# Decay exponents of the state-space pairs from stored running sums, inner products on row halves, and a new order inside a pair

## The reference

```
proj = u @ W_in.T                       # x|B|C (a causal convolution of 4 taps), z, A_log
a = -softplus(A_log).transpose(0, 2, 1) # one value per head and token
Lm = exp(segsum(a))                     # exp of the sum of a over (s, l], 0 for s > l
M = einsum('bhln,bhsn,bhls->bhls', Cm, Bm, Lm)   # C_l . B_s times the decay
y = einsum('bhls,bshp->blhp', M, x) + D * x
out = (y * silu(z + z_bias)) @ W_out.T
```

## Time and profile before

| | |
|---|---|
| median of 3 runs | 3554.8 us (3554.54 to 3561.59) |
| span of the profiled execution | 3547.7 us |
| PE busy | 3232.7 us, 91% |
| DVE busy | 2239.9 us, 63% |
| ACT busy | 1250.3 us, 35% |
| POOL busy | 1253.6 us, 35% |
| mean granted TensorE clock | 0.948 |

### The profile page before, as it was taken

How to read it: one execution, slowest core, us unless ns; L and a number is a source line. 1 busy time by engine, 2 the same in 40 slices (tenths; PEclk the granted TensorE clock), 3 DMA queues, 4 the chain that set the end, 5 groups by cost and what they waited for, 6 DMA issues and landing times.

```text
span 3547.7 us, 59609 instructions
## 1 busy us (share of the span) xinstructions
PE 3232.7 (91%) x20900; PEld 2219.6 (63%) x20900; DVE 2239.9 (63%) x2937; ACT 1250.3 (35%) x1904; POOL 1253.6 (35%) x1629
## 2 busy tenths in 40 slices
PE   3699989999789999999978999999997999899998
PEld 3445467777565447777655445777775454677775
DVE  1456676666646668666664766766665566776666
ACT  1133334444213323444412332444421333244442
POOL 1211114666221101666611111266642011146662
PEclk7789999999879999999987999999998899999999
DMA  7322101001212200011122320101112211011111
GB/s 244 104 66 54 36 12 34 30 30 36 75 48 54 65 13 24 29 30 30 31 78 54 71 49 1 30 30 32 35 35 78 65 43 48 10 30 36 30 36 45
DMA packets 121655, 166.69 MB, mean 47 GB/s; under 512 B 32224, under 2 KB 66656, under 8 KB 120864
## 3 DMA queue, kind: packets, MB, share of 16 engines
q1 hardware_dynamic: 117632, 151.11, 15.5%
q0 software_dynamic: 2720, 10.49, 0.7%
q10 hardware_dynamic: 1152, 3.15, 0.4%
HBM read 85.76 MB, written 19.92 MB: 30 GB/s over the span
## 4 chain that ended last, share of the span: by engine, by line
PE 79%; DVE 7%; issue 3%; DMA 3%; ACT 3%; SPq 2%; POOL 1%; ACTq 0%; DVEq 0%; POOLq 0%
PE ps L619 13%; PE ps L621 12%; PE ps L620 12%; PE ps L763 7%; PE ps L903 7%; PE ps L728 6%; PE ps L746 5%; PE ps L805 3%; PE ps L890 3%; PE ps L664 2%; PE ps L957 2%; DVE LM L1448 1%; PE ps L912 1%; DVE mneg L1374 1%; PE ps L629 1%
## 5 line engine op out<-in xcount | busy, mean ns | idle before, releaser
L619 PE MATMUL ps<-uh,win 128*128 128x512 f32 x1536 | 634.0, 413 | 0.0
L621 PE MATMUL ps<-uh,win 128*128 128x512 f32 x1536 | 604.1, 393 | 0.0
L620 PE MATMUL ps<-ul,win 128*128 128x512 f32 x1536 | 600.8, 391 | 0.0
L1374 DVE TENSOR_REDUCE mneg<-ps 128x1 f32<-128x128 f32 (+7 forms) x512 | 363.3, 752 | 174.9 <-PE ps L731 169.2
L1084 ACT ACTIVATE PR<-ps 128x1024 f32<-128x1024 f32 (+3 forms) x384 | 310.6, 810 | 405.8 <-PE ps L749 268.8
L1435 DVE SCALAR_TENSOR_TENSOR Bt<-ps,cpt,Bt 128x1023 f32<-128x1023 f32 (+2 forms) x192 | 246.0, 1281 | 206.7 <-ACT Bt L1145 202.1
L1626 POOL TENSOR_TENSOR OT<-OS,rec 64x512 f32 (+1 forms) x64 | 82.4, 1287 | 821.6 <-DVE rec L1387 821.6
L619 PEld LDWEIGHTS ps<-uh,win 128*128 128x128 f32 x1536 | 290.0, 189 | 97.9 <-issue 43.1
L1664 POOL TENSOR_TENSOR segh<-ah,tri 128x512 fp32r<-128x512 f32 x256 | 275.2, 1075 | 203.5 <-PE ps L890 203.5
L763 PE MATMUL ps<-PR,VG 128*32 128x512 f32 (+3 forms) x1536 | 337.0, 515 | 10.8 <-DVE OS L1380 8.3
L765 PE MATMUL ps<-PR,ones 128*32 128x512 f32 (+3 forms) x1536 | 337.0, 515 | 0.0
(11 more groups left out here) (207 smaller groups left out, 5977.9 us busy)
## 6 DMA issues: line engine op xcount, KB each, us to landing
win_raw<-in_t SPq DMA_DIRECT2D x160, 256.0 KB, 2.7
QS<-EV SPq DMA_DIRECT2D x192, 128.0 KB, 2.4
KS<-EV SPq DMA_DIRECT2D x168, 128.0 KB, 2.4
X<-in_L_attn_b_W_in_dram SPq DMA_DIRECT2D x10, 1024.0 KB, 7.7
in_t<-tiles POOLq DMA_DIRECT2D x10, 1024.0 KB, 8.1
win_raw<-in_L_attn_a_Wqkv_dram SPq DMA_DIRECT2D x34, 256.0 KB, 3.7
X<-in_L_attn_a_x_dram SPq DMA_DIRECT2D x32, 256.0 KB, 4.5
xh<-y SPq DMA_DIRECT2D x256, 32.0 KB, 1.9
```

What stands on the lines that cost most here:

```text
L619: pe.matmul(dst, hi_l, hi_r, start=first, stop=False)
L620: pe.matmul(dst, hi_l, lo_r, start=False, stop=False)
L621: return pe.matmul(dst, lo_l, hi_r, start=False, stop=last)
L1374: dve.tensor_reduce(mneg[:, hh, t:t + 1], wide(b0)[:, 0:(t + 1) * P], AX.X, ALU.max, negate=True).then_inc(a_max.sem, 1)
```

## The change

Ahead of the pairs of a batch, `a` is split into a coarse part (`a_1`, multiples of a grid) and the rest (`a_2`). `sums()` makes the running sums of both in each chunk by 16 matmuls; they are split again and stored in DRAM (`cum_dram`), and so is the exponent of the whole running sum (`ed_dram`), by 16 DMAs in `store_decays`.

In a pair, the exponent of the decay matrix comes from one matmul for each `segment(q)` with 100 rows: 32 rows of a staircase, which puts a large negative number above the diagonal's blocks of 4, 4 rows that add the sum at l, 64 rows that subtract the sum at s for each of 16 (head, chunk) columns. `sl` (stationary) and `sg` (moving) hold them; `pair_cums` loads what differs from pair to pair by four DMAs. `segh`, `segl` and `arep` go. `edec` is loaded by `pair_decay`: eight DMAs a pair, each for 16 partitions, out of one head's row copied to all of them.

The inner products take rows 0 to 63 and 64 to 127 of `Bt` and `Ct` for the two heads, 16 matmuls of 128 columns instead of 8 of 256, into two banks; `CD` goes. `LM` is now ordered by half and head.

The order in a pair changes on every engine. On ScalarE `pair_hi` of pair n + 2 moves from behind the copies of `dT` to ahead of `tap` and of the copy of `dS`. On TensorE the transposes of `dS` move ahead of `project_ahead(1, 0)`. VectorE's taps of B are spread over the pair. SyncE issues `pair_cums(j + 1)` ahead of `save_y(j)` and `pair_decay(j + 2)` behind it.

```diff
+GRID = 3072.0
+STEP = 4
+STAIRS = P // STEP
+CROWS = STAIRS + 4 + 4 * 2 * NC
+SEG_BANK = [6, 7, 7, 4]
...
+                def store_decays():
+                    cm_low.wait(sp, b, 1)
+                    for c4 in range(4):
+                        for h in range(2):
+                            rows_ = slice(c4 * NH + h * PAIRS, c4 * NH + (h + 1) * PAIRS)
+                            sp.dma_start(cum_dram.rearrange("j r (h e f) t -> j r h f e t", h=2, f=4)[:, :, h, c4],
+                                         cums[rows_, :, :].bitcast(F32).rearrange("p r (e t) -> p r e t", e=2)).then_inc(s_cumw, 16)
+                    ed_act.wait(sp, b, 1)
+                    for c4 in range(4):
+                        for h in range(2):
+                            rows_ = slice(c4 * NH + h * PAIRS, c4 * NH + (h + 1) * PAIRS)
+                            sp.dma_start(ed_dram.rearrange("(j h) (e f) t -> j h f e t", h=2, f=4)[:, h, c4],
+                                         eds[rows_, :].rearrange("p (e t) -> p e t", e=2)).then_inc(s_cumw, 16)
+                def pair_cums(j, par):
+                    one = bass.ds(j, 1)
+                    for g in range(2):
+                        at = STAIRS + g * (2 + 4 * NC)
+                        sp.dma_start(sg[par][at:at + 2, :].bitcast(F32),
+                                     cum_dram[one, 2 * g:2 * g + 2, :, :].rearrange("j r k t -> (j r) (k t)")).then_inc(s_cum[par], 16)
+                        sp.dma_start(sl[par][at + 2:at + 2 + 4 * NC, :].bitcast(F32),
+                                     cum_dram[one, 2 * g:2 * g + 2, :, :].rearrange("j r k t -> (j r k) t")).then_inc(s_cum[par], 16)
+                def pair_decay(j, par):
+                    two = bass.ds(j * 2, 2)
+                    for c4 in range(4):
+                        for h in range(2):
+                            at = c4 * 32 + h * HD
+                            src = ed_dram[bass.ds(j * 2 + h, 1), :, :].rearrange("h (e f) t -> h f e t", f=4)[:, c4]
+                            sp.dma_start(edec[at:at + HD, par, :, :],
+                                         src.rearrange("h e t -> (h e) t").partition_broadcast(HD)).then_inc(s_ed[par], 16)
...
+                    if t == 2:
+                        for par in range(2):
+                            sp.dma_start(sg[par][:, :].bitcast(F32), grid_dram).then_inc(s_grid, 16)
+                    if t == 4:
+                        store_decays()
+                    if t == 6:
+                        sp.wait_ge(s_cumw, b * 256 + 256)
+                        sp.wait_ge(s_grid, b * 32 + 32)
+                        pair_cums(0, 0)
+                        for par in range(2):
+                            pair_decay(par, par)
...
+                            if not (last and q == 3):
+                                pair_cums(j + 1, (q + 1) % 2)
                             save_y(j, q)
+                            if not (last and q >= 2):
+                                pair_decay(j + 2, q % 2)
...
+                def sums():
+                    cm_dve.wait(pe, b, 1)
+                    for k, src in enumerate((a_1, a_2)):
+                        for c in range(NC):
+                            rows_, cols = quarter(c)
+                            i = pe.matmul(ps[rows_, 7, cols.start + k * 2 * P:cols.stop + k * 2 * P], src[:, c, :, :].rearrange("p h j -> p (h j)"), tri[:, :],
+                                          start=True, stop=True)
+                    i.then_inc(cm_pe.sem, 1)
...
-                def mix(n, par, ahead):
+                def mix(n, par, ahead, occ):
                     def project_ahead(w, c):
                         if ahead is not None:
...
                     def segment(q):
-                        seg_pool.wait(pe, n, q + 1)
-                        if q == 1:
-                            ed_act.wait(pe, n, 1)
-                        if q >= 2:
-                            seg_act.wait(pe, n, q - 1)
-                        for part, src in enumerate((segh, segl)):
-                            i = pe.matmul(ps[:, 4 + 3 * (q % 2), :], after[:, :],
-                                          src[:, q % 2, :], start=(part == 0), stop=(part == 1))
-                        i.then_inc(seg_pe.sem, 1)
-                    def inner(q):
                         if q == 0:
-                            cd_act.wait(pe, n, 1)
-                        if q == 1:
+                            pe.wait_ge(s_cum[par], occ * 64 + 64)
+                        elif q == 1:
+                            bt_act.wait(pe, n, 2)
+                        elif q == 2:
+                            seg_act.wait(pe, n, 2)
+                        else:
                             dt_act.wait(pe, n, 1)
-                        if q >= 2:
-                            m_dve.wait(pe, n, q - 1)
-                        for c in (2 * q, 2 * q + 1):
-                            i = pe.matmul(ps[:, 5 + q % 2, (c % 2) * WIN:(c % 2 + 1) * WIN], Bt[:, par, c * P:(c + 1) * P],
-                                          CD[:, c, :, :].rearrange("p h t -> p (h t)"), start=True, stop=True)
+                        at = (q % 2) * L + (q // 2) * HB
+                        pe.matmul(ps[:, SEG_BANK[q], :], sl[par][:, :], sg[par][:, at:at + HB],
+                                  start=True, stop=True).then_inc(seg_pe.sem, 1)
+                    def inner(half):
+                        if half == 0:
+                            bc_dve.wait(pe, n, 2)
+                            seg_act.wait(pe, n, 1)
+                        else:
+                            m_dve.wait(pe, n, 2)
+                        for k in range(4):
+                            tok = slice((half * 4 + k) * P, (half * 4 + k + 1) * P)
+                            for h in range(2):
+                                hs = slice(h * NS, (h + 1) * NS)
+                                i = pe.matmul(ps[:, 5 + h, k * P:(k + 1) * P], Bt[hs, par, tok], Ct[hs, par, tok],
+                                              start=True, stop=True)
                         i.then_inc(g_pe.sem, 1)
                     project_ahead(0, 0)
...
                     bc_dve.wait(pe, n, 1)
                     y_dve.wait(pe, n, 0)
                     for c in range(NC):
-                        i = pe.transpose(ps[:, 4 + c // 4, (c % 4) * P:(c % 4 + 1) * P], Bt[:, par, c * P:(c + 1) * P], ident[:, :])
+                        i = pe.transpose(ps[:, 4 + 3 * (c // 4), (c % 4) * P:(c % 4 + 1) * P], Bt[:, par, c * P:(c + 1) * P], ident[:, :])
                         if c % 4 == 3:
                             i.then_inc(bt_pe.sem, 1)
-                    ar_pool.wait(pe, n, 1)
+                    segment(0)
+                    project_ahead(0, 1)
+                    bt_act.wait(pe, n, 2)
+                    xd_pool.wait(pe, n, 1)
                     for c in range(NC):
                         rows_, cols = quarter(c)
-                        i = pe.matmul(ps[rows_, 7, cols], arep[:, c, :, :].rearrange("p h q -> p (h q)"), tri[:, :], start=True, stop=True)
-                    i.then_inc(ed_pe.sem, 1)
-                    project_ahead(0, 1)
-                    bt_act.wait(pe, n, 2)
-                    for c in range(NC):
-                        rows_, cols = quarter(c)
-                        i = pe.matmul(ps[rows_, 6, cols], xd[:, c, :, :].rearrange("p h q -> p (h q)"), BT[:, c, :], start=True, stop=True)
+                        i = pe.matmul(ps[rows_, 4, cols], xd[:, c, :, :].rearrange("p h q -> p (h q)"), BT[:, c, :], start=True, stop=True)
                     i.then_inc(ds_pe.sem, 1)
-                    segment(0)
                     inner(0)
                     segment(1)
-                    project_ahead(1, 0)
                     ds_act.wait(pe, n, 1)
                     for a in range(2):
-                        i = pe.transpose(ps[:, 6, a * P:(a + 1) * P], dS[:, a, :], ident[:, :])
+                        i = pe.transpose(ps[:, 4, (2 + a) * P:(3 + a) * P], dS[:, a, :], ident[:, :])
                     i.then_inc(dt_pe.sem, 1)
+                    project_ahead(1, 0)
                     segment(2)
+                    segment(3)
                     inner(1)
-                    segment(3)
-                    inner(2)
-                    inner(3)
                     project_ahead(1, 1)
-                    seg_act.wait(pe, n, 3)
+                    seg_act.wait(pe, n, 4)
                     st_pool.wait(pe, n, 1)
...
-                                          LM[:, c // 2, ((c % 2) * 2 + h) * P:((c % 2) * 2 + h + 1) * P], start=(h == 0), stop=(h == 1))
+                                          LM[:, (c // 4) * 2 + h, (c % 4) * P:(c % 4 + 1) * P], start=(h == 0), stop=(h == 1))
                     i.then_inc(ya_pe.sem, 1)
...
+                        cm_pe.wait(act, b, 1)
+                        act.copy(cums[:, 0, :], ps[:, 7, 0:2 * P])
```

(96 more changed lines are left out.)

98 lines of the change are left out of this document (67 added, 31 removed).

## The result

The changed kernel takes 3719.8 us (median of 4 runs, 3710.25 to 3727.92) against 3554.67 (3550.42 to 3561.59, 4 runs) for the kernel before: a ratio of 1.0459, interval 1.0437 to 1.0482. It is slower, by 165 us. Predicted were 3685 us, 3500 to 3850. The profiled execution took 3710.25 us, its span is 3708.5, so 160.8 longer than the span before, and its mean granted clock is 0.912 instead of 0.948.

What follows compares the result with a forecast made beforehand. TensorE, busy 91% of the span, was taken to bound the kernel. 52 waiting pairs x 2.9 - 8 x 2.6 - 4 x 5 + 4 x 5 + 3 = +133 us on 3554.8 gave 3688, stated as 3685, range 3500 to 3850.

Steps and rivals of the forecast that it cites:

- What an issue costs: SyncE's queue: each of eight `pair_decay` issues ahead of the weights takes 0.50 us with its gap (0.38 to 0.63).
- When the weights land: Behind the eight issues, at 10.2 us (9.2 to 11.2) after T0, the first `save_y` issue of the pair before.
- TensorE turns `dS`: TensorE's transposes of `dS` wait for ScalarE's copy, done 13.0 us after T0.
- It stands idle: TensorE, ready at T0 + 8.3, waits 4.7 us for the copy of `dS`, where before nothing waited.
- From there to T0 without the clock: TensorE's work from the transposes of `dS` to the next T0: 9.8 us, with no clock loss counted.
- How many: Pairs that wait: 13 x 4 = 52; 8 others are free and 4 are last of a batch.
- The inner products: On TensorE, as row halves: 2.3 us a pair, between 1.55 side by side and 3.1 one after the other.
- the clock: TensorE's granted clock falls behind the idle gap in most pairs, costing 1.3 us a pair (0 to 2.8).
- A pair in which nothing waits: Pair time with work taken off TensorE and no new wait: 18.6 us (17.8 to 19.4), from 21.23.
- Issues that cost the queue nearly nothing: Rival, SyncE: weights land at T0 + 6.2, a pair takes 18.8 us, the kernel 3414 us; 14%.
- Loads of the halves that bind: Rival, inner products: 32 loads of 0.14 us, none overlapping, 4.5 us instead of 2.3; kernel 3770 us; 10%.
- A clock that stays low for all that follows: Rival, TensorE: some 10 us behind the gap at half speed, +8 us more a pair, kernel 4100 us; 4%.

Runs made afterwards that it cites:

- experiment 3: The changed kernel with 18 matmuls, their result overwritten, ahead of TensorE's wait for the copy of `dS`: 3654.04 us, ratio 1.0273 to the kernel before.
- experiment 5: Experiment 4's kernel with the inner products of a half ordered by head instead of alternating between heads: 3448.41 us, ratio 0.9681 to the kernel before.
- experiment 1: The changed kernel with SyncE's `pair_decay` moved from behind `save_y` to behind `pair_cums`, so behind the weights: 3408.05 us, ratio 0.9581 to the kernel before.
- experiment 7: The kernel before with eight spare loads like those of `edec` issued between `save_y` and the weights: 3558.25 us, ratio 0.9996.
- experiment 2: The changed kernel with `pair_hi` back behind the copies of `dT` and `pair_lo` back behind `masked(2)`: 3383.27 us, ratio 0.95 to the kernel before.
- experiment 4: The changed kernel with the weights of pair j + 3 issued ahead of `save_y` of pair j: 3376.86 us, ratio 0.9475 to the kernel before.

## Why the prediction was right, point by point

**The mechanism** held at each step, by the prediction's own marks:

- *What an issue costs* (0.50 with its gap, 0.38 to 0.63): 3.95 us for eight, 0.49 each. The instruction itself is shorter, 0.32 to 0.41 us in this pair; between two of them the trace has a register operation (0.04 to 0.05) and a move (0.03) on the same line, with short pauses. Together the weights go out 7.07 - 2.95 = 4.12 us later, 0.52 an issue. No reading is under the 0.3 us at which I would have been wrong.
- *When the weights land* (T0 + 10.2): ScalarE starts `win` at 10.35 in the pair shown, 10.6 on average over 52.
- *TensorE turns `dS`* at T0 + 13.0: measured 12.81 in the pair shown and 13.07 on average. *It stands idle* for 4.7 us: 248.1 / 52 = 4.77.
- *From there to T0 without the clock*, 9.8: 9.77 in the pairs that don't wait, 9.80 to 9.83 in experiment 3.
- *How many*: 52.
- *The inner products* (2.3 us a pair, 1.55 to 3.1): twice 1.09, 2.2. This was the middle of two ends, 1.55 and 3.1, and came out right for another reason: the passes do run side by side, and what is above 1.55 is the time at the start and end of each half of them, 2 x 0.2 us, and their spacing of 0.112. Of the two pages of the Trainium skill that stood for the ends, the trace agrees with "TensorEngine Tiling (Array Packing)" (section "Tiling Modes"), by which tiles load and multiply in parallel: two passes on different halves start 0.007 us apart (experiment 5). By "TensorE: Matmul & The Clock Gate" (section "LDWEIGHTS (loading the stationary operand)") a load of half the rows is no shorter; the trace does not speak against that, but loads do not add up here either, since 16 passes with 16 loads take 1.09 us.

**The term that was mis-sized is the clock**, "I take 1.3 us a pair". Experiment 3 gives 11.72 - 9.82 = 1.9. The two gaps of the earlier trace rows had lost 1.7 and 2.8 us; the prediction took less and spoke of most pairs, but none of the 52 kept the clock. A waiting pair is 24.79 us on average (23.8 to 26.0) and not 24.1. Against the 2.9 us a pair of the sum it is 24.79 - 21.25 = 3.54, 52 x 0.64 = 33 us more. What a pair loses follows the time at the lower level behind its gap: 2.7 us of it go with 11.05 us from the transposes to T0 (1.2 lost), 6.1 us with 12.59 (2.8 lost), so a little less than half. The part inside the gap costs nothing. Why the stretch is short in some pairs and twice as long in others of equal shape, no run here explains.

One mark of the prediction did not come: a granted clock near 0.8 in the pairs. It is 0.89 over the 52, since the lower level holds for 5.3 us of 24.8. At 0.8 it would be some 10 us a pair, which did not fit the 1.3 us of the sum either.

**The smaller terms.** A pair in which nothing waits takes 17.92 us, at the low end of 17.8 to 19.4 where I took 18.6: -3 us for the four pairs 14. The prediction's own stations gave another figure, 8.3 + 9.8 = 18.1, and measured are 8.14 + 9.77; the two sums should have been compared. The first pair's T0 is 589.57 after and 588.73 before, +0.8 where the sum has -2.6 + 5 + 3 = 5.4. From pair 14 to the next batch's first pair it is 557.7, 561.0 and 561.6 after, 562.8, 562.2 and 562.7 before, -2.4 on average where the sum has -5 + 5 - 2.6 = -2.6. That this agrees is in part luck. The last pair alone, from its T0 to its own `save_y`, goes from 17.46 to 14.17 us on average, -3.3 and not -5, and all the rest up to the next batch's first pair is 0.9 longer and not 2.4. Together: the sum's 133, +33 for the waiting pairs, -3, -5, and +2 left over for the last pair of the last batch and what follows, is 160, the difference of the spans.

**The rivals.** Issues that cost the queue nearly nothing: fell, 0.49 against the 0.30 at which it decides. It describes well what happens once the delay is gone: 3414 us were worked out for it, experiment 1 took 3408. The Trainium skill, "DMA: Bandwidth & Descriptors", section "Issuing engines are not separate DMA queues", calls the sequencer's time usually small beside the DMA. Here an issue takes 0.49 us of the queue and its load lands 1.6 us after it, so it is nearly a third; and the eight issues add up to 3.95 us. For these small loads the trace does not agree. Loads of the halves that bind: fell, 16 passes take 1.09 us, 0.068 each and not 0.14. A clock that stays low for all that follows: fell, it is 0.99 again from 656.5 on, and at most 6.1 us behind a gap are at the lower level.

**What only the experiments showed** is that the loss needs both moves. The late issue alone costs nothing (experiment 7 in the kernel before, and experiment 2 in the changed one: `pair_hi` comes late enough). The early split alone costs nothing in experiment 4 and 0.6 us a pair in experiment 1, where TensorE still waits 31.1 us in 52 pairs for `dS`. Undo either and the rest of the change is worth 4 to 5%, since a pair in which nothing waits is 3.3 us shorter than before.

## What to carry to other kernels

When an operation moves ahead on an in-order engine, compare the time at which it will now be reached with the time at which its transfer lands, and list what stands behind it. When small DMAs are added to a queue, count their spacing times their number against the slack of the big transfer behind them, and put the transfer that is wanted first ahead of the wait that it does not need. Do both sums with both changes in place: each alone fitted its slack, and a kernel in which every engine lost work became 4.6% slower.

## What the runs showed of the hardware that was not expected

- The half clock behind a gap of 4.2 to 5.5 us costs from 11.05 - 9.82 = 1.2 to 12.59 - 9.82 = 2.8 us in pairs that do the same work. It goes with the time at the lower level behind the gap, 2.7 to 6.1 us, and not with the length of the gap; what lies at the lower level inside the gap (1.15 us on average) is free. Filling the gap with 18 useless matmuls made the kernel faster, 1.0273 against 1.0459.
- Passes of 64 rows and 128 columns in float32 start in twos, 0.007 us apart, when they alternate between the row halves (and, here, banks), and one two follows another after 0.112 us; passes on the same half come every 0.111 us. A block of 16 takes 1.09 against 1.64 us.
- The loads of `edec`, 16 KB to 16 partitions with an address worked out at run time, occupy SyncE for 0.49 us each, of which the issue itself is 0.32 to 0.41.
